# Expert rows in 64 slots of 256 and 7 of 128, where there were 71 of 256

## The reference, cut to what matters

```python
xf = x.reshape(b * t, d)                       # 8192 x 256, layer-normed
logits = xf @ gate_w.T                         # 8 experts
topk_logits, topk_idx = jax.lax.top_k(logits, TOP_K)       # 2 of them
topk_w = jax.nn.softmax(topk_logits.astype(jnp.float32), axis=-1)
comb = jnp.zeros((N, E), x.dtype).at[jnp.arange(N)[:, None], topk_idx].add(topk_w)
for e in range(E):
    g = xf @ wg[e].T                           # 256 -> 384
    u = xf @ wu[e].T
    y = jax.nn.silu(g) * u @ w_down[e].T       # 384 -> 256
    out = out + comb[:, e:e + 1] * y
shared = jax.nn.silu(xf @ sg_gate.T) * (xf @ sg_up.T) @ sg_down.T
```

## Time and profile before

| | us |
|---|---|
| median of three runs (1745.64 to 1747.42) | 1746.89 |
| the profiled execution | 1744.85 |
| its span, first to last instruction | 1742.7 |

### The profile page before, as it was taken

How to read it: one execution, slowest core, us unless ns; L and a number is a source line. 1 busy time by engine, 2 the same in 40 slices (tenths; PEclk the granted TensorE clock), 3 DMA queues, 4 the chain that set the end, 5 groups by cost and what they waited for, 6 DMA issues and landing times.

```text
span 1742.7 us, 25628 instructions
## 1 busy us (share of the span) xinstructions
PE 1680.7 (96%) x7243; PEld 1227.5 (70%) x7289; DVE 1166.9 (67%) x1968; ACT 904.1 (52%) x2240; POOL 1166.9 (67%) x624
## 2 busy tenths in 40 slices
PE   6899999999999999999999998989999999999997
PEld 4555666666666666666666665578888888888886
DVE  7989999999999999999999993322222222222221
ACT  4356667667667667667667646522322322332322
POOL 5769889889889889889889881413333343343343
PEclk9898999999999999999999999999999999999999
DMA  4302211211211211111111111367777777777764
GB/s 151 116 13 61 62 49 37 62 49 36 61 49 36 61 49 36 59 50 36 54 55 37 37 49 37 92 169 162 165 154 160 165 157 156 167 158 156 168 158 78
DMA packets 89455, 157.20 MB, mean 90 GB/s; under 512 B 8896, under 2 KB 72128, under 8 KB 89024
## 3 DMA queue, kind: packets, MB, share of 16 engines
q1 hardware_dynamic: 60512, 112.58, 20.9%
q0 software_dynamic: 28896, 44.06, 14.9%
HBM read 101.79 MB, written 48.56 MB: 86 GB/s over the span
## 4 chain that ended last, share of the span: by engine, by line
PE 89%; ACT 5%; DVE 2%; issue 2%; DMA 1%; POOL 1%; SPq 1%; POOLq 0%; ACTq 0%; DVEq 0%
PE p_b L1494 17%; PE p_b L1548 13%; PE p_b L1698 10%; PE p_b L1709 10%; PE p_b L1641 8%; PE p_q L1698 7%; PE p_q L1466 6%; PE p_v L1698 4%; PE p_v L1466 3%; PE p_b L1480 2%; PE p_xT L1685 2%; PE p_xT L1626 2%; ACT rows L706 1%; ACT xmid L706 1%; PE p_b L1588 1%
## 5 line engine op out<-in xcount | busy, mean ns | idle before, releaser
L654 POOL DMA_INDIRECT out_rows<-prod_pool,prod x142 | 221.4, 1559 | 387.9 <-ACT prod_pool L949 357.5
L523 POOL TENSOR_TENSOR prod_pool<-prod_pool 128x2048 f32<-128x2048 f32 (+1 forms) x180 | 347.9, 1933 | 14.1
L1548 PE MATMUL p_b<-bT,fc_sb 128*128 128x512 f32 x512 | 231.5, 606 | 1.3 <-ACT bT L865 1.3
L1494 PE MATMUL p_b<-proj_sb,hid 128*128 128x256 f32 x1024 | 230.5, 379 | 0.0
L1494 PEld LDWEIGHTS p_b<-proj_sb,hid 128*128 128x128 f32 x1024 | 189.6, 190 | 29.4 <-issue 0.5
L1026 DVE TENSOR_TENSOR prod<-p_q,eqk 128x4096 f32<-128x4096 f32 (+1 forms) x47 | 184.0, 3914 | 5.3 <-DVE attn L1076 1.0
L1698 PE MATMUL p_b<-prod,exp_up 128*128 128x256 f32 x840 | 187.1, 379 | 0.0
L1063 DVE TENSOR_REDUCE qkv<-prod 128x256 f32<-128x4096 f32 (+1 forms) x47 | 183.7, 3910 | 1.6
L1050 DVE TENSOR_TENSOR prod<-p_q,v_dve 128x2048 f32<-128x2048 f32 (+2 forms) x60 | 177.4, 2956 | 1.5
L574 POOL DMA_INDIRECT rows_sorted<-rows,slot x128 | 125.7, 982 | 78.5 <-issue 34.5
L1035 DVE TENSOR_REDUCE p_q<-prod 128x128 f32<-128x2048 f32 (+2 forms) x60 | 177.4, 2957 | 1.1
(11 more groups left out here) (208 smaller groups left out, 2988.6 us busy)
## 6 DMA issues: line engine op xcount, KB each, us to landing
exp_up<-in_experts SPq DMA_DIRECT2D x71, 768.0 KB
prod<-rows_sorted SPq DMA_DIRECT2D x71, 260.0 KB
xin<-in_x SPq DMA_DIRECT2D x16, 512.0 KB, 3.4
xres<-in_x SPq DMA_DIRECT2D x16, 512.0 KB
xres<-xmid POOLq DMA_DIRECT2D x16, 512.0 KB, 4.6
out_rows<-x SPq DMA_DIRECT2D x16, 512.0 KB, 2.9
exp_dn<-in_experts SPq DMA_DIRECT2D x8, 384.0 KB, 5.8
out_rows<-prod_pool,prod POOLq DMA_INDIRECT x142, 3.8
```

What stands on the lines that cost most here:

```text
L523: done(g.tensor_tensor(prod_pool[:, at:at + n * w], prod_pool[:, at:at + n * w], prod_pool[:, at + n * w:at + 2 * n * w], ALU.add))
L654: pool.indirect_dma_start(out=out[:, :], out_offset=bass.IndirectOffsetOnAxis(ap=tok_i[j][:, a:a + 1], axis=0), in_=yg[j][:, a * D:(a + 1) ...
L1494: ins = t_.matmul(o, src[:, k, t * P:(t + 1) * P], w[:, k, :], start=k == 0, stop=bias_at is None and k == chunks - 1)
L1548: ins = t_.matmul(bnk[:], fc_sb[:, k, f * P:(f + 1) * P], bT[:, k, :], start=k == 0, stop=k == KC - 1)
```

## The change

The number of rows of an expert is now counted in pieces of 128. Pairs of them fill the wide slots (`WIDE` = 64), in the order of the experts. An odd piece that is left over, at most one for each expert, goes to a slot of its own: to a wide slot that the pairs leave free, or to one of 7 narrow slots of 128 rows behind them (`SLOTS` = 71 in all). Where there are more than 64 pairs, the pairs beyond are split over two narrow slots each. The tables therefore need more steps on VectorE and more constants, which POOL makes (two iotas, nine memsets). The table of waits `tab_wait` is gone: the first add of a slot always waits for the second add of the slot before. In the narrow slots each engine does its operations for one half only: the load of rows has 128 of them, the transposes are 2, the matmuls of gate_up have 128 columns, down has 6 matmuls, and there is one weigh and one add. The load of weights is the same. The narrow slots are written out on all engines, behind loops over wide slots (slots 2 to 61 on PE and ACT, 2 to 63 on the others). The spare rows in `rows_sorted` are 256 where they were 2048.

```diff
@@ -48,8 +48,10 @@
 SUB = 2
 TILE = SUB * P
 REGION = TOKENS + TILE
-SORTED_TILES = 2 * TOKENS // TILE + EXPERTS - 1
-SPARE_TILES = EXPERTS
+WIDE = 2 * TOKENS // TILE
+SLOTS = WIDE + EXPERTS - 1
+TABLE = WIDE + EXPERTS
+SPARE_TILES = 1
...
+        def halves(k):
+            return SUB if not isinstance(k, int) or k < WIDE else 1
+        def rows_of_slots(n):
+            return SUB * n if not isinstance(n, int) or n <= WIDE else SUB * WIDE + n - WIDE
+        def adds(h, n):
+            return 16 * (n if h == 0 or not isinstance(n, int) else min(n, WIDE))
...
             def load(k, j):
                 row = sp.value_load(tab_row[0:1, bass.ds(k, 1)], min_val=0,
-                                    max_val=EXPERTS * REGION + (SPARE_TILES - 1) * TILE)
+                                    max_val=EXPERTS * REGION)
                 wait(sp, gT_psum, k - 1)
                 wait(sp, xg_meta, k - 1)
-                sp.dma_start(xg[j], rows_sorted[bass.ds(row, TILE), :].rearrange("(a p) r -> p a r", p=P)
+                n = halves(k)
+                sp.dma_start(xg[j][:, 0:n, :], rows_sorted[bass.ds(row, n * P), :].rearrange("(a p) r -> p a r", p=P)
                              ).then_inc(xg_loaded[j], 16)
...
-            with sp.Fori(1, SORTED_TILES // 2) as m:
+            with sp.Fori(1, WIDE // 2) as m:
                 load(2 * m, 0)
                 load_up(2 * m, 0)
                 load(2 * m + 1, 1)
                 load_up(2 * m + 1, 1)
-            load(SORTED_TILES - 1, 0)
-            load_up(SORTED_TILES - 1, 0)
+            for k in range(WIDE, SLOTS):
+                load(k, k % 2)
+                load_up(k, k % 2)
             sp.wait_ge(out_stored, 16 * BLOCKS)
-            for j in range(2):
-                sp.wait_ge(added[j], 16 * SORTED_TILES)
+            sp.wait_ge(added[0], 16 * SLOTS)
+            sp.wait_ge(added[1], 16 * WIDE)
...
-                    g.iota(iota_k, [[1, SORTED_TILES]], base=0, channel_multiplier=0,
+                    g.iota(slot_i, [[1, TABLE]], base=-WIDE, channel_multiplier=0,
                            allow_small_or_imprecise_dtypes=True).then_inc(pool_const, 1)
-                    g.iota(iota_w, [[16, SORTED_TILES + 1]], base=0, channel_multiplier=0,
-                           allow_small_or_imprecise_dtypes=True).then_inc(pool_const, 1)
+                    done.later(g.iota(slot_q[:, 0:WIDE], [[1, WIDE]], base=0, channel_multiplier=0,
+                                      allow_small_or_imprecise_dtypes=True))
+                    done(g.memset(slot_half, 0.0))
+                    for i in range(EXPERTS // 2):
+                        at = WIDE + 2 * i
+                        done.later(g.memset(slot_q[:, at:at + 2], float(WIDE + i)))
+                        done.later(g.memset(slot_half[:, at + 1:at + 2], float(P)))
+                    done.sync()
+                    pool.sem_inc(pool_const, 1)
...
             def add(k, j):
-                if isinstance(k, int):
-                    before = 16 * k
-                else:
-                    before = pool.value_load(tab_wait[0:1, bass.ds(k, 1)], min_val=16, max_val=16 * SORTED_TILES)
-                for a in range(SUB):
-                    pool.wait_ge(y_ready, SUB * k + a + 1)
-                    wait(pool, added[a], 16 * k)
+                for a in range(halves(k)):
+                    pool.wait_ge(y_ready, rows_of_slots(k) + a + 1)
+                    wait(pool, added[a], adds(a, k))
                     if a == 0:
-                        wait(pool, added[1], before)
+                        wait(pool, added[1], adds(1, k))
                     stand_alone(pool)
...
             def take_gT(k, j):
                 act.wait_ge(gT_psum, k + 1)
                 wait(act, gu_psum, HCH * (k - 1))
-                a.activation(xgT[j], p_xT[:], ACT.Copy).then_inc(gT_ready, 1)
+                n = KC * halves(k) * P
+                a.activation(xgT[j][:, 0:n], p_xT[:, 0:n], ACT.Copy).then_inc(gT_ready, 1)
...
-                for h in range(SUB):
-                    wait(act, added[h], 16 * (k - 1))
+                for h in range(halves(k)):
+                    wait(act, added[h], adds(h, k - 1))
                     a.activation(yg[j][:, h * D:(h + 1) * D], y_bank[:, h * D:(h + 1) * D], ACT.Copy,
...
             def tables():
                 announce(dve, v.tensor_scalar(pad_at[:], free_row[:], iota_p[:, 0:1], None, ALU.add), pads_at, 1)
...
+                pairs, singles = parts_of[:, 0, :], parts_of[:, 1, :]
+                done(v.tensor_tensor(subs_f, free_row[:], iota_r[:], ALU.subtract))
+                done(v.tensor_scalar(cnt_i, subs_f, float(P - 1), None, ALU.add))
+                done(v.tensor_scalar(cnt_i, cnt_i, P.bit_length() - 1, None, ALU.arith_shift_right))
+                done(v.tensor_copy(subs_f, cnt_i))
+                done(v.tensor_scalar(cnt_i, cnt_i, 1, None, ALU.arith_shift_right))
+                done(v.tensor_copy(pairs, cnt_i))
+                done(v.scalar_tensor_tensor(singles, pairs, -2.0, subs_f, ALU.mult, ALU.add))
+                done(v.tensor_copy(parts_to, parts_of))
                 for e in range(1, EXPERTS):
...
+                    done(v.tensor_tensor(parts_to[:, :, e:e + 1], parts_to[:, :, e:e + 1], parts_to[:, :, e - 1:e],
+                                         ALU.add))
+                over, one = (prod[:, lo:lo + TABLE * EXPERTS].rearrange("p (k e) -> p k e", e=EXPERTS)
+                             for lo in (0, TABLE * EXPERTS))
+                wide = [P, TABLE, EXPERTS]
+                def by_slot(z):
+                    return z.unsqueeze(2).to_broadcast(wide)
+                def by_expert(z):
+                    return z.unsqueeze(1).to_broadcast(wide)
+                def choose_from(at, yes, no):
+                    done(v.tensor_tensor(at, yes, no, ALU.subtract))
+                    done(v.tensor_tensor(at, at, is_wide, ALU.mult))
+                    done(v.tensor_tensor(at, at, no, ALU.add))
+                done(v.tensor_scalar(lacking, parts_to[:, 0, EXPERTS - 1:], -1.0, None, ALU.mult))
+                done(v.tensor_scalar(lacking, lacking, float(WIDE), None, ALU.add))
+                done(v.tensor_scalar(shift, lacking, 0.0, None, ALU.min))
+                done(v.tensor_tensor(shift, shift, lacking, ALU.add))
                 dve.wait_ge(pool_const, 8)
...
+                done(v.tensor_scalar(slot_i, slot_i, shift[:, 0:1], None, ALU.add))
+                done.later(v.tensor_tensor(over, by_slot(slot_q), by_expert(parts_to[:, 0, :]), ALU.is_ge))
+                done(v.tensor_tensor(one, by_slot(slot_i), by_expert(parts_to[:, 1, :]), ALU.is_ge))
+                done.later(v.tensor_reduce(e_wide, over, AX.X, ALU.add))
+                done(v.tensor_reduce(e_one, one, AX.X, ALU.add))
+                done.later(v.tensor_tensor(over, over, by_expert(pairs), ALU.mult))
+                done(v.tensor_tensor(one, by_expert(iota_e[:]), by_slot(e_one), ALU.is_equal))
+                done.later(v.tensor_reduce(first_of, over, AX.X, ALU.add))
+                done(v.tensor_tensor(one, one, by_expert(pairs), ALU.mult))
+                done.later(v.tensor_reduce(one_of, one, AX.X, ALU.add))
+                done(v.tensor_scalar(is_wide, e_wide, float(EXPERTS), None, ALU.is_lt))
+                choose_from(tab_e, e_wide, e_one)
                 done(v.tensor_scalar(tab_ei, tab_e, float(EXPERTS - 1), None, ALU.min))
...
+                done(v.tensor_tensor(first_of, slot_q, first_of, ALU.subtract))
+                done(v.scalar_tensor_tensor(first_of, first_of, float(TILE), slot_half, ALU.mult, ALU.add))
+                done(v.tensor_scalar(one_of, one_of, float(TILE), None, ALU.mult))
+                choose_from(slot_q, first_of, one_of)
+                v.scalar_tensor_tensor(tab_row, tab_e, float(REGION), slot_q, ALU.mult, ALU.add
                                        ).then_inc(tables_ready, 1)
...
             def meta_weights(k, j):
                 for h in range(SUB):
-                    wait(dve, added[h], 16 * (k - 1))
+                    wait(dve, added[h], adds(h, k - 1))
...
                     for part in range(2):
                         for c in range(KC):
                             at = c * 2 * HALF + part * HALF + i * P
-                            ins = t_.matmul(gu_banks[j][i][:, part * TILE:(part + 1) * TILE],
-                                            exp_up[j][:, at:at + P], xgT[j][:, c * TILE:(c + 1) * TILE],
+                            n = halves(k) * P
+                            ins = t_.matmul(gu_banks[j][i][:, part * n:(part + 1) * n],
+                                            exp_up[j][:, at:at + P], xgT[j][:, c * n:(c + 1) * n],
                                             start=c == 0, stop=c == KC - 1)
...
             def down(k, j, e):
                 pe.wait_ge(hg_ready, HCH * (k + 1))
-                wait(pe, y_ready, SUB * k)
-                for h in range(SUB):
```

(28 more changed lines are left out.)

65 lines of the change are left out of this document (21 added, 44 removed).

## The result

| | before | after |
|---|---|---|
| median, us | 1747.16 | 1725.01 |
| lowest to highest | 1745.64 to 1748.04 | 1723.30 to 1728.14 |
| the profiled execution, its span | 1744.85, 1742.7 | 1728.14, 1726.4 |

The ratio is 0.9876, with a 95% interval of 0.9859 to 0.9893: 22 us faster. The forecast was 1722.0 with a range of 1712 to 1731. The profiled execution of the kernel after is the slowest of its four. So I also use profiles of the same kernel from three later runs.

A forecast was written before the change was run, and what follows sets the result against it. TensorE's 71 slots and a tail of adds set the end; narrow slots go at the adds' pace. Narrow slots -24.7, contention +1.5, entry -2.0 give 1719.7 us, plus 2.04 for the median: 1722, range 1712 to 1731.

The forecast's parts named there:

- Wide slots at nothing: In wide slots the full wait of the first add costs nothing, with 2.5 us to spare.
- The narrow slot on TensorE: Transposes, gate_up and down of a narrow slot: 0.22 + 2.64 + 1.30 = 4.16 us.
- the rival of 6.7 us: Narrow gate_up: weight load and matmul follow each other, 6.7 us a slot, 1727 us in all; chance 0.07.
- the last of the 16 pairs of the earlier trace: Load-and-matmul pairs in the kernel before: 1.92 us, last matmul's latency about 0.17, hence 0.117 us a pair.
- The adds set the pace: Narrow slots: each add waits for the one before to land, 4.64 us a slot; end 24.7 us earlier.
- Contention of 1.5 us: Narrow slots: weight loads crowd DMA and delay adds, between 0 and 5 us, taken as 1.5.
- Tables 14.3 us, hidden: VectorE's longer tables take 14.3 us, to 1132.5, hidden behind SyncE's pad copies with 0.5 us to spare.
- Entry gain of 2.0 us: Before the first slot: TensorE's long gap moves ahead of the last shared down, first slot avoids clock 0.50; 2.0 us gained.
- The constants on POOL at nothing: Two iotas and nine memsets on POOL lie in an 11.6 us gap; cost nothing, bounds 0 and 2 us.
- Sum: Whole kernel: -24.7 + 1.5 - 2.0 = -25.2 us on the profiled execution's 1744.85.
- The likeliest case: The forecast itself, 1722 us with adds setting the narrow slots' pace; chance 0.62.
- The slower rival: Wide slots: the first add's full wait bites once landings exceed 6.3 us; 1765 us at 7 us landings; chance 0.03.

The follow-up runs named there:

- after_again: The kernel after, unchanged, run again for a second profile: 1721.84 us, ratio 0.9872 to the kernel before.
- long_tables: The kernel before with eight more compares of 568 elements at the end of the tables, results unused: 1741.11 us, ratio 0.9990.
- after_third: The kernel after, unchanged, run a third time beside the reordered kernels: 1722.85 us, ratio 0.9883 to the kernel before.
- after_fourth: The kernel after, unchanged, run beside a version with slot 63's wait relaxed: 1723.47 us, ratio 0.9870 to the kernel before.
- narrow_first: The kernel after with its 7 narrow slots at the start and the 64 wide ones behind: 1724.83 us, ratio 0.9898 to the kernel before.
- interleaved: The kernel after with one narrow slot behind every nine wide ones, in a loop over ten: 1762.50 us, ratio 1.0118 to the kernel before.

## Why the prediction was right, and where a term was off

- **Wide slots at nothing: right.** A slot is 8.21 us in both kernels, the margin of the full wait held, and removing the lookup alone changed nothing in the slots (589.13 us against 589.22).
- **The narrow slot on TensorE: right.** The 24 matmuls of 128 columns take 2.84 us with the last one's latency, 1677.98 to 1680.66 from start to start of the next group: 2.68 against 2.64 predicted. Load and matmul don't follow each other; the rival of 6.7 us is out. The rule of the Trainium skill quoted for it ("TensorE: Matmul & The Clock Gate", Part 3, "What overlaps and what doesn't") did not hold for these matmuls of all rows: a pair comes every 0.112 us, less than the 0.19 us that its weight load takes. The slot was priced at full clock alone: behind a wait a narrow gate_up can take longer, as the one from 1705.64 to 1709.48 us, 3.84 us at a granted clock of 0.68. While the adds set the pace this costs little.
- **One reading there was off, without effect.** The prediction took the last of the 16 pairs of the earlier trace rows as 0.17 us long and so 0.117 us a pair. That matmul is 0.26 us long, and the pairs start every 0.112 us, as the narrow slot's do.
- **The adds set the pace: right.** Predicted 4.64 us a slot; 4.5 to 4.6 without the weight loads in all periods but one, and -24.95 us for the whole against -24.7.
- **Contention of 1.5 us: mis-sized.** It is 3.1 to 3.7 us in three profiles, reckoned from -24.7, and 6.6 in the first, above the bound of 5. The step that failed is "the last two slots have no loads behind them and the median is near the low end": I spread the landings of the earlier trace rows over the narrow slots. But the stretch isn't even. Most of the price arises where wide turns to narrow: in after_again the second add of slot 62 and the first of 63 are 6.48 us apart (1671.47, 1677.95) and the second of 63 and that of 64 6.06 (1679.82, 1685.88), where the prediction had 4.6 for both. That is 3.3 of the 3.65 us; the three periods behind them are 4.77 to 5.20, and the last three are 4.6 or less. In all four profiles the weight load goes out 0.2 to 0.3 us ahead of these two second adds, and they land in 5.7 to 6.4 and 4.8 to 5.2 us. I also had counted the DMA engines' load (92%) and not the moment: the shorter gate_up moves the weight load onto the second add. In the first profile one further add landed after 6.46 us though its load went out 1.5 us behind it, as far as behind others that landed in 3.8 to 4.6. What that one met isn't known.
- **Tables 14.3 us, hidden: right.** They took 14.15 (1117.82 to 1131.97), and long_tables shows that such a length is free.
- **Entry gain of 2.0 us: right in one profile (-2.45), 0.6 to 1.3 in two, and a loss of 1.8 in the first.** The gap moved ahead of the shared down, as predicted, in after_again and after_third (3.56 and 3.91 us there, 0.32 and none ahead of the first transposes), and not in after_fourth (1.41 and 3.08), whose 1.27 us must come from elsewhere. Nor did it in the first profile. In that one ScalarE stood for 3.82 us ahead of a copy, which held the last matmuls ahead of the shared down, so the gap ahead of that down stayed at 1.46 us and the long gap and the clock of 0.5 stayed where they were before. Why ScalarE stood isn't settled. The loss itself goes with the pad copies, whose end the prediction took as fixed at 1132.99 us: SyncE ended them at 1134.39, so the first loads went out 1.4 us later and the first transposes started 1.7 us later. The pad copies took 10.5 to 15.0 us in the traces of all kernels here, so the entry varies by some microseconds in either kernel.
- **The constants on POOL at nothing: right.** They end at 1098.89 us, 11.28 us ahead of POOL's next operation.
- **Sum.** With contention 3.4 and an entry gain of 1, the kernel gains 22.3 us, and the medians of the four comparisons gained 20.4 to 22.7. The likeliest case was the right one, and both misses lie on the same side.
- **The slower rival** had the right mechanism for wide slots, that a late landing holds the first add of the next slot: narrow_first meets it for the rest of its run, interleaved at every group. In the kernel after no wide slot ahead of the junction meets it. At slots 63 and 64 the first add waits for a landing already in the prediction's sum; what it had too low there is the landing.

## What to carry to other kernels

Where a transfer on one queue is released by one engine and an accumulating write by another, look at the distance between the two in the timeline, not only at how full the DMA engines are: a shorter piece of work moves the one against the other. Keep unlike pieces together: seven short slots at the end gained 22 us, at the start 18, and the same seven spread out lost 19. A wait with 2.5 us to spare is free only as long as no landing of 3.8 us grows past 6.3, and a single delay may then be enough to keep it late, as in the one profile of narrow_first.

## What the runs showed of the hardware

- An add of 128 rows lands in 3.8 us in the middle if a 768 KB load goes out 2.2 to 2.4 us behind it (3.7 to 3.9 in the kernel before, once 4.4 in after_again). With the load from 0.3 us ahead to 1.0 us behind it takes 4.7 to 8.3 us over all runs here, 6.4 in the middle of 83 such adds; the 8.3 is in the interleaved kernel, with the load 0.7 us behind. With the load 1.5 to 1.7 us behind it takes 3.9 us in the middle, but 5.3 to 7.0 in six of 51 cases. By which shared part of the DMA path isn't shown. The Trainium skill says ("DMA: Bandwidth & Descriptors", "Queues, rings and completion order") that each DMA engine goes round between its queues packet by packet; adds that wait for their turn among the load's packets would fit, but no run here isolates it.
- The same loop over wide slots can keep two paces: 8.21 us a slot, and 9.5 in the mean of six slots of narrow_first once load and add meet. The slow one need not last: in the interleaved kernel it ended after two slots behind each of the first five narrow slots and lasted behind the sixth.
- From a landing to the next add's issue are 0.77 us (1675.72 + 5.74 to 1682.23) or 0.87 (1684.10 + 5.02 to 1689.99), the latter as in the earlier trace rows.
